# Perceiver block on one core: key lengths per token, a new order of the recurrence's projections, value rows ahead of the recurrence, and experts that gather their tokens

## The reference, cut to what matters

```python
# second step: the recurrence
q, k, v = silu(x @ Wq), silu(x @ Wk), x @ Wv          # 16 heads of 16
log_f = log_sigmoid(x @ Wf1 @ Wf2); gamma = -sigmoid(x @ Wgamma)
k = k / max(norm(k, per head), 1e-12)
a = k * gamma[..., None] * exp(log_f)
# per token: S = S * f; S = S + k (a.S_old*f + v); o = q.S   (64 tokens in sequence)
o = layer_norm_of(o * sigmoid(x @ Wog1 @ Wog2)) @ Wo
# third step: self-attention, then the experts (T = 1024 tokens, 8 experts, C = 256 rows each)
top1, top2 = the two experts with the largest logits of each token
s1, s2 = the token's running place in its expert; places from C on are dropped
buf[top1, s1] = x; buf[top2, s2] = x
y = relu(buf @ w1 + b1) @ w2 + b2                      # per expert, 256 -> 1024 -> 256
out = g1 * y[top1, s1] + g2 * y[top2, s2]
```

## Time and profile before

| | us |
|---|---|
| median of 3 runs (lowest, highest) | 994.61 (992.96, 995.33) |
| the profiled execution's own time | 992.36 |
| its span, first to last instruction | 990.6 |
| mean granted clock of TensorE | 0.898 |
| busy: PE, DVE, ACT, POOL | 841.5, 589.6, 430.1, 339.4 |
| first instruction of the projections | 170.08 |
| first instruction of the recurrence | 228.00 |
| first instruction of the experts' stage | 521.83 |
| clock in 170 to 178, 178 to 200, 200 to 225 | 0.58, 0.89, 0.84 |
| clock in 225 to 235, 235 to 402 | 0.50, 1.00 |
| clock in 521.7 to 561.5, 561.5 to 680 | 0.50 to 0.53, 0.98 |

### The profile page before, as it was taken

How to read it: one execution, slowest core, us unless ns; L and a number is a source line. 1 busy time by engine, 2 the same in 40 slices (tenths; PEclk the granted TensorE clock), 3 DMA queues, 4 the chain that set the end, 5 groups by cost and what they waited for, 6 DMA issues and landing times. The chain is left out here.

```text
span 990.6 us, 19998 instructions
## 1 busy us (share of the span) xinstructions
PE 841.5 (85%) x7396; PEld 631.3 (64%) x7396; DVE 589.6 (60%) x1374; ACT 430.1 (43%) x1245; POOL 339.4 (34%) x466
## 2 busy tenths in 40 slices
PE   5999997975999999759685399994789996687998
PEld 4888885434999999635464288883567773464344
DVE  3555556376999999671857032233696775463751
ACT  3666564657644550135444000000476663663730
POOL 2112111046999999210332800003533331250000
PEclk9999999887999999768795599997599997798999
DMA  7113500000000000000200255534353200000001
GB/s 237 31 33 102 187 13 2 1 0 1 1 1 2 1 1 1 1 1 0 87 2 28 85 159 172 189 107 143 110 153 90 73 24 0 2 3 1 1 1 43
DMA packets 45284, 51.72 MB, mean 52 GB/s; under 512 B 7205, under 2 KB 40850, under 8 KB 45060
## 3 DMA queue, kind: packets, MB, share of 16 engines
q1 hardware_dynamic: 40644, 43.47, 13.9%
q0 software_dynamic: 1536, 4.08, 1.3%
q10 hardware_dynamic: 3008, 2.88, 0.8%
HBM read 43.20 MB, written 7.34 MB: 51 GB/s over the span
## 5 line engine op out<-in xcount | busy, mean ns | idle before, releaser
L656 POOL TENSOR_TENSOR r_faded<-r_state,rec_f 128x256 f32<-128x256 f32 x128 | 82.1, 642 | 17.5 <-DVE r_state L635 7.2
L683 PE MATMUL r_u_ps<-r_t_in,l_same_head 128*128 128x256 f32 x256 | 87.1, 422 | 0.2
L662 POOL TENSOR_TENSOR r_q_in<-r_state,rec_q 128x256 f32<-128x256 f32 x128 | 82.1, 641 | 0.3 <-DVE r_state L635 0.2
L690 PEld LDWEIGHTS r_o_ps<-l_head_of,r_q_in 128*128 128x128 f32 x512 | 77.3, 192 | 6.9 <-POOL r_q_in L662 0.4
L1360 ACT ACTIVATE a_prob<-a_s_ps,a_negmax 128x256 f32<-128x256 f32 x128 | 59.0, 488 | 41.2 <-DVE a_negmax L1397 41.2
L1020 ACT ACTIVATE a_prob<-a_s_ps,a_negmax 128x256 f32<-128x256 f32 x128 | 59.1, 486 | 19.7 <-DVE a_negmax L1076 19.7
L690 PE MATMUL r_o_ps<-l_head_of,r_q_in 128*128 128x8 f32 x512 | 65.4, 236 | 0.3 <-POOL r_q_in L662 0.3
L628 DVE TENSOR_TENSOR r_update<-r_u_ps,rec_k 128x256 f32<-128x256 f32 x128 | 55.2, 431 | 6.8 <-PE r_u_ps L683 6.8
L1896 PE MATMUL m_h_ps<-m_rowsT,l_w 128*128 128x256 f32 x256 | 58.2, 387 | 0.3 <-ACT m_rowsT L1939 0.3
L1818 DVE TENSOR_SCALAR m_hidden<-m_h_ps,l_b 128x256 f32<-128x256 f32 x64 | 28.0, 479 | 48.7 <-PE m_h_ps L1896 48.7
L635 DVE TENSOR_TENSOR r_state<-r_update,r_faded 128x256 f32<-128x256 f32 x128 | 54.3, 424 | 4.4
(11 more groups left out here) (321 smaller groups left out, 1983.2 us busy)
## 6 DMA issues: line engine op xcount, KB each, us to landing
l_w<-in_B_w SPq DMA_DIRECT2D x16, 1024.0 KB, 6.0
a_ctxT<-in_ctxT SPq DMA_DIRECT2D x31, 256.0 KB, 2.8
a_ctx<-in_ctx SPq DMA_DIRECT2D x16, 256.0 KB, 3.2
expert_rows<-ffn_zeros SPq DMA_DIRECT2D x8, 256.0 KB, 2.9
m_rows<-expert_rows SPq DMA_DIRECT2D x8, 256.0 KB, 5.9
expert_out<-m_y ACTq DMA_DIRECT2D x7, 256.0 KB, 6.5
all_X<-in_x SPq DMA_DIRECT2D x4, 256.0 KB, 5.4
l_b<-in_B_b SPq DMA_DIRECT2D x1, 1024.0 KB
```

The source lines that it names most:

```text
L656: nc.gpsimd.tensor_tensor(faded[m][:, :, :], state[(t + 1) % 2][m][:, :, :], row("f", t, m), ALU.mult).then_inc(faded_ready[m], 1)
L662: nc.gpsimd.tensor_tensor(q_in[t % 2][m][:, :, :], state[t % 2][m][:, :, :], row("q", t, m), ALU.mult).then_inc(q_ready[m], 1)
L683: nc.tensor.matmul(u_ps[t % 2][m][:, 0:B, :], same_head[:, :], t_in[m][:, :, :], start=False, stop=True).then_inc(u_mm[m], 1)
L690: mm = nc.tensor.matmul(o_ps[:, 2 * m + c, :, t % U], q_in[t % 2][m][:, c * (B // 2):(c + 1) * (B // 2), :], head_of[:, :], start=True, st ...
```

## The change

1. **Key lengths.** PE sums the squares with the squares as the stationary side and `head_of` (8 columns) as the moving one, so the sums stand by token, 128x8 per tile (`sums`); ScalarE takes roots of 128x32 right behind q1 (`lengths`), DVE clips and inverts 128x32 and copies the result over the 16 places of a head (`wide`), and products with `ident` spread it back (`spread`, behind f1). DVE reads that from PSUM to scale k.
2. **Order of the products.** In each half the gates come behind q1, then g and f, and v last. v is read by DVE instead of ScalarE. GpSimd makes f*f and the query product; gamma enters on DVE (`gated_units`, `decays`).
3. **First value rows.** Rows 0 are made at the end of the projections, eight by ScalarE and eight by DVE, into QT; the recurrence makes rows 1 and 2 before its loop.
4. **Experts.** No cleared buffer and no scatter. SP stores the 8 tiles of normed rows to HBM plainly. DVE forms for every token and choice a one-hot of its row within 128 (`row_hot`, bf16) and of its part, expert and upper or lower 128 (`part_hot`), the latter times the token's number in two terms. PE's product of the two gives, for every row of every expert, the token that belongs there; GpSimd gathers the rows by it, two transfers per expert, four of them before its scaling of b2 and its sums X += Y, twelve behind. DVE's choices begin when all tiles are normed, and ScalarE's roots move ahead of its reads of turned tiles.

The diff, cut to its core:

```diff
-RJOBS = ("k0", "k1", "low", "q0", "q1", "g0", "f0", "v0", "v1", "g1", "f1", "gate0", "gate1")
+RJOBS = [(c, name) for c in range(2) for name in ("k0", "k1", "low", "q0", "q1", "gate0", "gate1", "g0", "f0", "g1", "f1", "v0", "v1")]
...
                 def inverse_lengths(c, m):
+                    dve.wait_ge(n_taken, ONE + KD * c + m + 1)
+                    nc.vector.tensor_scalar(length[:, c, m, :, :], length[:, c, m, :, :], 1e-12, None, ALU.max).then_inc(len_ready, 1)
                     dve.wait_ge(len_ready, ONE + KD * c + m + 1)
-                    nc.vector.reciprocal(r["k_sig"][:, m, cols(c)], r["k_sig"][:, m, cols(c)]).then_inc(n_ready, 1)
+                    nc.vector.reciprocal(inverse[:, c, m, :, :], length[:, c, m, :, :]).then_inc(inv_ready, 1)
+                    dve.wait_ge(inv_ready, ONE + KD * c + m + 1)
+                    nc.vector.tensor_copy(wide[:, c, m, :, :, :], inverse[:, c, m, :, :].unsqueeze(3).to_broadcast([P, CH, HH, HD])).then_inc(n_ready, 1)
...
+                def values(c, m):
+                    dve.wait_ge(acc_mm, ONE + RJOBS.index((c, f"v{m}")) + 1)
+                    nc.vector.tensor_copy(r["v"][:, m, cols(c)], acc[RJOBS.index((c, f"v{m}")) % RING][:, :]).then_inc(v_read, 1)
...
+                dve.wait_ge(v_read, ONE + 2 * KD)
+                for i in range(1, HD, 2):
+                    nc.vector.tensor_scalar(first_out(i), first_v, diag[:, i:i + 1], None, ALU.mult).then_inc(rows_ready, 1)
...
+                def sums(c, m):
...
+                    for j in range(CH):
+                        t = CH * c + j
+                        mm = nc.tensor.matmul(n_ps[m][:, (CH * c + j) * HH:(CH * c + j + 1) * HH], r["a"][:, m, t * P:(t + 1) * P], head_of[:, :], start=True, stop=True)
+                    mm.then_inc(n_mm, 1)
+
+                def spread(c, m):
...
+                    for j in range(CH):
+                        mm = nc.tensor.matmul(n_ps[m][:, j * P:(j + 1) * P], wide[:, c, m, j, :, :].rearrange("p h k -> p (h k)"), ident[:, :], start=True, stop=True)
+                    mm.then_inc(spread_mm, 1)
...
                         if name in ("q0", "q1"):
+                            sums(c, int(name[1]))
+                        if name == "f1":
+                            spread(c, 0)
+                            spread(c, 1)
...
                 def values(t, m):
-                    pe.wait_ge(v_ready, ONE + HD * (t // V + 1))
+                    if t >= V:
+                        pe.wait_ge(v_ready, ONE + HD * (t // V))
...
                 parameters(0)
-                for n in range(3):
+                for n in range(1, 3):
                     value_rows(n)
...
-                pool.wait_ge(*cleared)
-                for t in range(NT):
-                    pool.wait_ge(kept_ready, ONE + t // 2 + 1)
-                    scatter(t, 0)
-                pool.wait_ge(kept_ready, ONE + NT // 2 + 1)
-                for t in range(NT):
-                    scatter(t, 1)
+                def gather_rows(e):
+                    if e >= 2:
+                        pool.wait_ge(xt_mm, ONE + e - 1)
+                    for c in range(2):
+                        nc.gpsimd.indirect_dma_start(out=rows[e % 2][:, c, :], out_offset=None, in_=xn_d, in_offset=bass.IndirectOffsetOnAxis(ap=token[:, 2 * e + c:2 * e + c + 1], axis=0)).then_inc(rows_in[e % 2], 16)
+
+                pool.wait_ge(stored, ONE + 16 * NT)
+                pool.wait_ge(token_ready, ONE + 1)
+                gather_rows(0)
+                gather_rows(1)
                 nc.gpsimd.tensor_scalar(b2[:, :, :], b2[:, :, :], 1.0 - DROPOUT, None, ALU.mult).then_inc(b2_ready, 1)
                 for t in range(NT):
                     nc.gpsimd.tensor_tensor(X[:, t, :], X[:, t, :], Y[:, t, :], ALU.add).then_inc(x_summed, 1)
+                for e in range(2, E):
+                    gather_rows(e)
...
+                def tokens(ts, c):
+                    pe.wait_ge(hot_ready, ONE + (ts.stop // 2 if c == 0 else NT // 2 + 1))
+                    for t in range(ts.start, ts.stop):
+                        mm = nc.tensor.matmul(token_ps, row_hot[:, t, c, :], token_hot[:, t, c, :, :], start=(c == 0 and t == 0), stop=(c == 1 and t == NT - 1))
...
+                for g in range(NT // 2):
+                    tokens(slice(2 * g, 2 * g + 2), 0)
+                tokens(slice(0, NT), 1)
                 turn_rows(0)
                 turn_rows(1)
...
-                sp.wait_ge(scattered, 16 * 2 * NT)
-                load_rows(0)
-                load_rows(1)
-                load_rows(2)
+                for t in range(NT):
+                    sp.wait_ge(normed.scaled, ONE + t + 1)
+                    sp.dma_start(xn_d[t * P:(t + 1) * P, :], xn[:, t, :]).then_inc(stored, 16)
                 load_first(2)
```

More of the change, by code:

```diff
@@ L347, in _ @@
                     pe.wait_ge(normed.taken, ONE + 4 * c + 4)
-                    for i, name in enumerate(RJOBS):
-                        product(c, i, name)
+                    for i, name in enumerate(name for half, name in RJOBS if half == c):
+                        product(c, name)
                         if c == 0 and i < 4:
@@ L1475, in _, with batch_attention_stage @@
                 add(NT - 1)
[L1478 removed]
+def batch_attention_stage(nc, stage, X, QT, KT, vblk, ident, WoT, bo, ones, limit=None, scale=1.0, rotary=None):
     NU = NT // 2
@@ L1710, in moe_stage @@
         count = sc.sb("count", [P, NT, 2, E])
-        place, over, row, top2, fits = (sc.sb(n, [P, NT, 2]) for n in ("place", "over", "row", "top2", "fits"))
+        place, over, upper, row, part_at, top2, fits = (sc.sb(n, [P, NT, 2]) for n in ("place", "over", "upper", "row", "part_at", "top2", "fits"))
+        row_hot = sc.sb("row_hot", [P, NT, 2, P], BF16)
+        part_hot = sc.sb("part_hot", [P, NT, 2, PARTS])
+        token_hot = sc.sb("token_hot", [P, NT, 2, 2, PARTS], BF16)
+        token_sum = sc.sb("token_sum", [P, PARTS])
+        token = sc.sb("token", [P, PARTS], U32)
+        token_ps = xt_ps[1][:, 0, 0:2 * PARTS].rearrange("p (i h) -> p i h", i=2)
+        row_no, part_no, place_no, tile_no = route[:, 0:P], route[:, P:P + PARTS], route[:, P + PARTS:P + PARTS + 1], route[:, P + PARTS + 1:P + PARTS + 1 + NT]
         firsts = sc.sb("firsts", [P, NT])
@@ L1945, in store_rows @@
                         act.dma_start(expert_rows(y_d, e, c.start, c.stop), y[e % 2][:, c, :]).then_inc(y_out[e % 2], 16)
-                for g in range(NT // 2):
-                    normed.roots(act, g)
-                    if g >= 1:
-                        normed.take(act, 2 * g - 2)
-                        normed.take(act, 2 * g - 1)
-                normed.take(act, NT - 2)
-                normed.take(act, NT - 1)
+                normed.roots(act, 0)
+                for t in range(NT):
+                    if t + 1 < NT // 2:
+                        normed.roots(act, t + 1)
+                    normed.take(act, t)
                 act.wait_ge(shift_ready, ONE + 2)
```

215 lines of the change are left out of this document (115 added, 100 removed).

## The result

The changed kernel takes 986.87 us (median of 5 runs, 984.32 to 988.64), the kernel before 994.74 (992.96 to 997.25) beside it: ratio 0.9918, 95% interval 0.9893 to 0.9942. The forecast was 987.8, faster. Spans therefore show less of the gain (3.8) than medians do (7.9), and I compare stage by stage.

The account below looks back on a forecast made before the run. Two stretches bound it: projections up to the recurrence's first update, and PE's wait for the experts' rows. Routing -6.5 and the middle -0.3 (+4.8, -5.1) sum to -6.8: 987.8 us against the median 994.61, range 981.5 to 994.7.

Parts of the forecast that it names:

- Routing, -6.5: Experts' routing: gathers replace scatters and a load, so the first layer starts at about 557.3 instead of 563.84, -6.5 us.
- The tokens: Routing: after DVE's choices, places and hot rows and PE's last products, the tokens stand at 547.3 to 547.8.
- The landing: Routing: a gather of 128 rows lands 3.8 us behind its issue, so the fourth is in at 556.4.
- the step on the order: Routing: without the late scaling, DVE's last logits come by 537.2, not 538.86; if no earlier, this would cost 1.7 us.
- Projections, +4.8: Projections: with the new product order and clock falls in both halves, the stage ends at 232.8 against 228.0, +4.8 us.
- q1 starts at 187.43 + 0.25: Projections, first half: q1 starts 0.25 us later, since eight 8-column passes (0.16 each) replace two 512-column ones (0.43 each).
- Recurrence, -5.1: Recurrence's start: no wait for value rows, so the first update comes 3.1 us behind the stage's start instead of 8.2, -5.1.
- A: The forecast: in the projections the clock falls in both halves and comes back inside v0 or v1; 987.8 us, chance 0.50.
- B: Rival, projections: the clock stays at 2.4 GHz, -5.9 us for projections and recurrence together; 982.2 us, chance 0.17.
- D: Rival, projections: half clock until v1 ends, in both halves, +6.6 us; 994.7 us, no change, chance 0.10.
- E: Rival, projections: half clock goes on into the next half's k0, k1, low and q0, 3.4 us; 998 us, chance 0.08.
- C: Rival, routing gains little: compares and landings at their dear ends, -1.7 us; 992.6 us, chance 0.15.

Follow-up runs that it names:

- e6: Changed kernel with DVE's choices and first places mixed back into the normalization loop: 987.46 us, ratio 0.9965 to the kernel before.
- e0: The changed kernel run again without an edit: 986.18 us, ratio 0.9923 to the kernel before.
- e5: Changed kernel with four unread 128-row products filling PE's wait behind f0 in each half: 979.27 us, ratio 0.9886 to the kernel before.
- e9: Changed kernel with v0 and v1 between q1 and the gates, DVE's v copies and value rows ahead of unit keys: 978.18 us, ratio 0.9843 to the kernel before.
- e10: e9 with the second expert's rows turned inside the first expert's first layer: 979.79 us, ratio 0.9860 to the kernel before.
- e11: Changed kernel with four unread 16-row products behind f0 in each half, filling PE's wait: 992.52 us, ratio 0.9975 to the kernel before.

## Why the prediction was right

**The bound.** That both stretches set the end, and nothing behind them moves, held: from the recurrence's first update to the experts' stage the two traces differ by 0.05 us, and from the first expert's second layer to the context attention's first turned tile by 0.1.

**Routing, -6.5, measured -8.3 in the stage and -8.4 as a kernel of its own.** The mechanism is the one given, mis-sized by two terms of 0.9. The tokens: DVE's compares cost 0.42 and 1.22 as taken from the earlier trace rows, and the last logits were copied 15.35 behind the stage's start (forecast 15.4). The prediction's own sum gives 547.3, 25.5 behind the start, and it used 547.8; that spare 0.5 was not needed, and the small operations took some 0.4 less than reckoned. The landing: 2.9 instead of 3.8. The median 3.8 of the earlier trace rows was taken in a stage where SP's loads share the queues; here nothing else runs, though that this is the reason was not tested. By the Trainium skill, DMA: Bandwidth & Descriptors, Anatomy of one DMA, the estimate for these bytes is 2.3; the trace stands between the two. Of the step on the order I had said that DVE's early scaling is worth 1.7 if the logits come no earlier; e6 prices it at 5.3, in DVE's waits. The forecast didn't need that number, since it timed the new order itself.

**Projections, +4.8, measured +3.1 to the stage's end.** From g1's start to the second half it forecast 9.8 to 10.3 and took 9.96; the second half 28.3 and 28.1. The step that failed is "q1 starts at 187.43 + 0.25". It starts 16.3 behind the stage's start (17.2 in e0) instead of 17.6: the eight passes of 8 columns take 0.81 where two of 512 took 0.86, so the sign of the 0.25 was wrong, and the rest is when the clock comes back in k1, which differs between profiles of one kernel: its four passes took 1.88 in this profile and 2.56 in e0's.

**Recurrence, -5.1, measured -5.25.** As reckoned.

**The clock.** A was right in each half: it falls and is back inside v. B came true only where full products stood in the gap (e5, e9), and not each time (e10). The Trainium skill, TensorE: Matmul & The Clock Gate, HAM oscillation, advises to do all products of a tile before a wait, so that the clock stays high. The trace agrees that the clock fell at a wait, of 1.86 us, and that a spreading at half clock costs 1.7 more. But the wait is not the whole matter: e11 has none and its clock fell in the same slice, and so did e10's behind full products. That section's account is of waits; that light stretches speak for D or E was my reading of it and not its words. D and E did not come: the clock was back inside v in each half.

**The sum**, -0.3 for the middle part, was too careful by 1.6 and the routing by 1.8. Together they would have put the median 3.4 lower; it came only 0.9 lower. The 2.5 between may be the context attention or the draw of the executions, which no run here separates. That the forecast lies so near is thus partly luck: two errors on the same side, and an unforeseen loss against them. Two slips in the working change nothing: B's first half ends at 201.6 by its own terms, not 201.4, and two thirds of C's chance is 0.10.

## What to carry to other kernels

Where PE must wait for a table load or a small operation, look for full products whose result another engine than the waiting one reads, and put them there: the wait, the copies behind it and, in one profile of two, the clock were worth 8.7 us here (7.1 in e10), about as much as the whole change. Let an engine that feeds a chain over three others (scale, turn, copy, logits) do all of that first and its own long work afterwards. Profile the same kernel more than once before you price a change of 1 us by a stretch that begins at half clock: the first layer alone took 14.8 to 16.3 us in three profiles of one kernel.

## What was new about the hardware

- Products of 16 rows do not keep TensorE's clock up: back to back with light ones before it (e11, PE busy 2.00 of 2.00), the clock was 0.57 in 194 to 196 us and 0.50 from 196 (0.73 and 0.50 in the kernel that waited there).
- The same products in the same order can be passed at either clock: with no wait of PE in either, the light stretch and the spreading behind v ran at 1.00 in e9, and the spreading at 0.56 in 198 to 200 us in e10.
- PE stopped for 1.0 to 1.6 us in all, in two or three parts with no releaser, within one group of 64 products of the untouched context attention: in nine of the fourteen profiles, each time 18.8 to 20.3 us behind the stage's first turned tile, with old and new routing, and in none of the four of one chip. Of that attention and the experts together, (c), 261.0 to 264.8 us are the range with the stop and 256.4 to 260.1 without it.
- One indirect gather of 128 rows of 1 KB was used by PE 2.9 us behind its issue with idle queues (2.8 to 5.7 in the earlier trace rows).
